# A 5x5 depthwise convolution split between GpSimd, beside the attention, and VectorE and TensorE, ahead of it

## What is computed

```python
xn = layer_norm(x, ln1_g, ln1_b)
q, k, v = xn @ q_w + q_b, (xn @ k_w + k_b) * scaling, xn @ v_w + v_b
lepe = dwconv(v, lepe_w, lepe_b)          # depthwise, 5 x 5, 'SAME', one filter per channel
qr, kr = theta_shift(q, sin, cos), theta_shift(k, sin, cos)   # 12 heads of 8 channels
attn = softmax(einsum("bnld,bnmd->bnlm", qr, kr) + mask)      # L = 1024 tokens
o = einsum("bnlm,bnmd->bnld", attn, v) + lepe
x = x + (o @ out_w + out_b)
```

## Time and profile before

| what | us |
|---|---|
| median of three runs | 3670.02 |
| the three runs | 3669.94, 3670.02, 3678.01 |
| the profiled execution, its own time | 3670.32 |
| its span, first to last instruction | 3668.7 |
| v projections, before the convolution (from 195.2) | to 219.95 |
| `depthwise` for `lepe` | 220.2 to 297.3 |
| attention, with its start and end | 297.9 to 1050.5 |

### The profile page before, as it was taken

How to read it: one execution, slowest core, us unless ns; L and a number is a source line. 1 busy time by engine, 2 the same in 40 slices (tenths; PEclk the granted TensorE clock), 3 DMA queues, 4 the chain that set the end, 5 groups by cost and what they waited for, 6 DMA issues and landing times. The chain is left out here.

```text
span 3668.7 us, 136690 instructions
## 1 busy us (share of the span) xinstructions
PE 3141.9 (86%) x50394; PEld 2339.4 (64%) x50394; DVE 2582.0 (70%) x12076; ACT 1821.7 (50%) x5594; POOL 583.8 (16%) x2420
## 2 busy tenths in 40 slices
PE   5378999999958947999999999999999998577787
PEld 1134666566622315888988888889888887254454
DVE  4567999999974635777777777777777778466562
ACT  2215999999933025444544444444444445133342
POOL 0001111111100001222222222222222222111110
PEclk9678999999978966555555555555555555678888
DMA  1312333333330000000000000000000000000000
GB/s 32 108 47 95 108 107 107 107 107 107 108 91 1 10 7 2 5 5 5 5 5 5 5 5 5 5 5 5 5 5 5 5 5 4 11 1 1 0 5 13
DMA packets 54608, 116.12 MB, mean 32 GB/s; under 512 B 12313, under 2 KB 19801, under 8 KB 53692
## 3 DMA queue, kind: packets, MB, share of 16 engines
q1 hardware_dynamic: 37104, 53.42, 5.3%
q0 software_dynamic: 13824, 50.34, 3.9%
q10 hardware_dynamic: 2956, 3.15, 0.4%
HBM read 84.06 MB, written 22.81 MB: 29 GB/s over the span
## 5 line engine op out<-in xcount | busy, mean ns | idle before, releaser
L504 PE MATMUL g_zr<-g_hp,g_wp 97*128 97x4 f16 x24576 | 1082.6, 171 | 53.4 <-issue 49.0
L504 PEld LDWEIGHTS g_zr<-g_hp,g_wp 97*128 97x128 f16 x24576 | 956.4, 108 | 157.4 <-issue 51.3
L595 ACT ACTIVATE g_e<-g_tn 96x8 f32<-96x8 f32 x2048 | 437.0, 213 | 557.8 <-DVE g_tn L540 557.8
L480 PE MATMUL g_zr<-s_inner,g_wi 96*128 (+2 forms) x6240 | 585.1, 234 | 61.9 <-issue 39.7
L612 POOL COPY s_y<-g_hs 96x8 f32 x2048 | 401.0, 196 | 1374.9 <-DVE g_hs L555 1374.9
L553 DVE TENSOR_TENSOR_SCAN g_hp<-g_gates,g_e 96x16 f16<-96x16 f32 x2048 | 382.1, 187 | 316.7 <-ACT g_e L595 207.6
L592 ACT ACTIVATE g_gates<-g_zr 96x16 f32<-96x16 f32 x2048 | 399.5, 195 | 315.5 <-PE g_zr L504 315.4
L511 PE MATMUL g_n<-g_hp,g_wp 97*128 97x8 f16 x8192 | 520.1, 174 | 0.0
L844 DVE CUSTOM_DVE_ANT_0 a_negated<-a_scores,a_mask 128x1024 f32<-128x1024 f32 x384 | 468.0, 1219 | 59.1 <-PE a_scores L762 41.2
L870 ACT ACTIVATE a_probs<-a_negated,a_negmax 128x1024 f32<-128x1024 f32 x384 | 442.4, 1152 | 26.1 <-DVE a_negmax L844 16.3
L540 DVE TENSOR_TENSOR_SCAN g_tn<-g_gates,g_n 96x24 f32<-96x24 f32 x2048 | 387.8, 189 | 95.7 <-ACT g_gates L592 95.7
(11 more groups left out here) (324 smaller groups left out, 3058.5 us busy)
## 6 DMA issues: line engine op xcount, KB each, us to landing
a_mask<-in_L_mask POOLq DMA_DIRECT2D x96, 512.0 KB, 5.6
a_k<-k_rows SPq DMA_DIRECT2D x96, 144.0 KB
q_rows<-r_q_parts SPq DMA_DIRECT2D x12, 576.0 KB, 7.4
k_rows<-r_k_parts SPq DMA_DIRECT2D x12, 576.0 KB, 7.4
a_q<-q_rows SPq DMA_DIRECT2D x96, 72.0 KB
o_parts<-a_o_sb SPq DMA_DIRECT2D x384, 18.0 KB
o_part<-o_parts SPq DMA_DIRECT2D x32, 192.0 KB
out_x<-x SPq DMA_DIRECT2D x4, 384.0 KB, 3.0
```

The costliest lines, as they stand in the source:

```text
L480: pe.matmul(o, wi[0:K, half, pw, d * NG + g, :], x, start=first, stop=False, skip_group_check=True)
L504: mm = pe.matmul(zr_bank[u, k][:, 1 - g, d, :, at], wp[0:97, part, (2 * u + d) * NG + g, :], hp[u][0:97, d * NB:(d + 1) * NB, e], start=False,
L595: act.activation(e1[u][:, :, 0], tn[u][:, :, 2], ACT.Tanh, scale=to_tanh).then_inc(n_and_zh[u], 1)
```

## The change

The convolution's work is divided anew, by image.

- **Images 2 and 3** stay in `depthwise`, ahead of the attention: of their four half images two go to TensorE (`on_tensor` is 2), and image 2 goes to VectorE.
- **Images 0 and 1** (`BESIDE`): ScalarE starts `lepe` with bias and centre tap (12) by an ACTIVATE for each, at the end of the token stage. The other 24 taps are done by GpSimd inside the attention, one tap of one image in each group whose image is 0 or 1: 48 groups, `convolve(2 * h + half, b, g)`. Each is a TENSOR_SCALAR into `term` and a TENSOR_TENSOR that adds it to `lepe`, with a wait between (`convolved`).
- GpSimd's `v` copy of a group waits for the convolutions of the groups before it, and its twelve heads are all written out, where ten ran in a loop.
- `vpad` and `lepe_w` are kept in memory through the attention.

The diff, cut to its core:

```diff
-def depthwise(nc, tag, jobs, size, on_tensor):
+def depthwise(nc, tag, jobs, size, on_tensor, batch=tuple(range(NB))):
-    work = [(k, b, half) for k in range(len(jobs)) for b in range(NB) for half in range(2)]
+    work = [(k, b, half) for k in range(len(jobs)) for b in batch for half in range(2)]
...
+BESIDE = (0, 1)
+OTHER_TAPS = [tap for tap in range(25) if tap != 12]
...
                         po.sem_inc(v_may, 1)
+                        po.wait_ge(convolved, done(g))
                         po.tensor_copy(vs[b % 2][:, :, 0:8], head).then_inc(v_ok, 1)
                         if b == 1 and not (half == 0 and first) and not (last and half == 1):
                             mask_load(h if half == 0 else h + 1, 1 - half, True)
-            heads(po, body)
+                        if b in BESIDE:
+                            convolve(2 * h + half, b, g)
+
+            def done(g):
+
+                return 2 * sum(i % NB in BESIDE for i in range(g))
+
+            def convolve(n, b, g):
+
+                tap = OTHER_TAPS[n]
+                dy, dx = tap // 5, tap % 5
+                image = lepe[:, cols(b)].rearrange("c (y x) -> c y x", y=HH)
+                po.wait_ge(v_ok, g + 1)
+                po.tensor_scalar(term[:, :, :], vpad[:, b, dy:dy + HH, dx:dx + HH], lepe_w[:, tap:tap + 1], None,
+                                 ALU.mult).then_inc(convolved, 1)
+                po.wait_ge(convolved, done(g) + 1)
+                po.tensor_tensor(image, image, term[:, :, :], ALU.add).then_inc(convolved, 1)
+
+            for h in range(NH):
+                body(h, h == 0, h == NH - 1)
...
                             act.activation(vt[:, i // 2, (i % 2) * 4:(i % 2) * 4 + 4, :], tokens[i % 2][:, :, 0:C],
                                            ACT.Copy).then_inc(taken, 1)
+                    for b in BESIDE:
+                        act.activation(lepe[:, cols(b)].rearrange("c (y x) -> c y x", y=HH),
+                                       vpad[:, b, 2:2 + HH, 2:2 + HH], ACT.Identity, bias=v["L0_lepe_b"][:, :],
+                                       scale=lepe_w[:, 12:13])
-                depthwise(nc, "r_lepe", [(vpad, lepe_w[:, :], v["L0_lepe_b"][:, :], None, lepe)], 5, 3)
+            depthwise(nc, "r_lepe", [(vpad, lepe_w[:, :], v["L0_lepe_b"][:, :], None, lepe)], 5, 2,
+                      tuple(b for b in range(NB) if b not in BESIDE))
```

More of the change, by code:

```diff
@@ L275, in _ @@
                 padded, taps, bias, addend, out = jobs[k]
-                images = [(b, HALF * sum((k, b, half) in own for half in range(2))) for b in range(NB)]
+                images = [(b, HALF * sum((k, b, half) in own for half in range(2))) for b in batch]
                 images = [(b, rows) for b, rows in images if rows]
@@ L619, with attention @@
 LAG = 2
-def attention(nc, mask, q_rows, k_rows, v_tokens, o_parts):
+BESIDE = (0, 1)
+OTHER_TAPS = [tap for tap in range(25) if tap != 12]
+def attention(nc, mask, q_rows, k_rows, v_tokens, o_parts, vpad, lepe, lepe_w):
     with ExitStack() as ctx:
@@ L639, in attention @@
         ident = sb("ident", [128, 128])
+        term = sb("term", [C, HH, HH])
+        convolved = sem("convolved")
         scores = [ctx.enter_context(nc.psum_tensor(f"a_scores{i}", [128, L], F)) for i in range(2)]
@@ L995, in retention_block @@
         lepe = outer.enter_context(nc.sbuf_tensor("r_lepe", [C, N], F))
+        lepe_w = outer.enter_context(nc.sbuf_tensor("r_lepe_w", [C, 25], F))
+        vpad = outer.enter_context(nc.sbuf_tensor("r_vpad", [C, NB, HH + 4, HH + 4], F))
         vt = outer.enter_context(nc.sbuf_tensor("r_vt", [128, NB, 8, C], F))
@@ L1095, in retention_block @@
                     sends += 3 * NB
[L1097 to L1110, removed]
-                    def _(pe):
-                        for i in range(N // BANK):
-                            if i >= 2:
-                                pe.wait_ge(taken, i - 1)
-                            for k in range(4):
-                                t = i * BANK + k * 128
-                                mm = pe.matmul(tokens[i % 2][:, k, 0:C], xn[:, t:t + 128], vw[:, :], start=True,
-                                               stop=True)
-                            mm.then_inc(made, 1)
-                    @block.scalar
-                    def _(act):
-                        for i in range(N // BANK):
-                            act.wait_ge(made, i + 1)
-                            act.activation(vt[:, i // 2, (i % 2) * 4:(i % 2) * 4 + 4, :], tokens[i % 2][:, :, 0:C],
-                                           ACT.Copy).then_inc(taken, 1)
-                depthwise(nc, "r_lepe", [(vpad, lepe_w[:, :], v["L0_lepe_b"][:, :], None, lepe)], 5, 3)
@@ L1131, in _ @@
                     sp.wait_ge(sent, 16 * sends)
-        attention(nc, d["L0_mask"], q_rows, k_rows, vt, o_parts)
+        attention(nc, d["L0_mask"], q_rows, k_rows, vt, o_parts, vpad, lepe, lepe_w)
         recycle(nc)
```

28 lines of the change are left out of this document (27 added, 1 removed).

## The result

The changed kernel takes **3638.26 us** (median of four runs, 3638.13 to 3641.11), the kernel before, run beside it, 3669.98 (four runs, 3667.72 to 3678.01). The ratio is 0.9912, its 95% interval 0.9894 to 0.9929. 12 us are missing from the sum.

What follows compares the result with a forecast made beforehand. The prediction took TensorE to bound `depthwise`, and TensorE, VectorE and ScalarE in a ring to bound the attention. Terms -21.8 and +2.2, others 0, sum to -19.6 against 3670.3; from the median 3670.0 it forecast 3650.4 us, range 3645 to 3672.

Steps and rivals of the forecast that it cites:

- The half image: In `depthwise`, TensorE does two half images instead of three, so its last eviction comes 21.78 us earlier: -21.8 us.
- The two ACTIVATEs: At the token stage's end, ScalarE starting images 0 and 1 holds the barrier: +2.2 us, bounds 1.95 and 2.30.
- The clock term: At the start of `depthwise`, TensorE's low-clock stretch after idling stays as costly: 0, bounds -3.1 and +3.1 us.
- VectorE did not come last: In `depthwise`, VectorE's image 2 takes at most 34 us against TensorE's 55; late only past 2.1 us a tap.
- GpSimd's pairs cost 0: In the attention, 48 pairs of 3.8 us each, at most 4.9, fit GpSimd's free time: 0 us.
- Rival A: In the attention, GpSimd's pairs hold back VectorE's custom instruction, 2.3 us a pair, 110 us: 3760 us; chance 0.12.
- B: In the attention, GpSimd is too slow and values come late; at 20 us a pair 3963 us; chance 0.02.
- C: In the attention, q loads come late more often beside the mask's traffic: +15.8 us, 3666 us; chance 0.05.
- D: In the attention, every pair costs someone 0.2 to 0.5 us, 17 us in all: about 3667 us; chance 0.08.
- a TENSOR_SCALAR at 1.28 us: In GpSimd's pair, the TENSOR_SCALAR costs as much as an AFFINE_SELECT, 1.28 us, at most the TENSOR_TENSOR's 2.36.
- GpSimd keeps up in each group: In the attention, GpSimd has 4.0 of 7.5 us to do without the mask, 6.1 with it, 7.2 at the bound.
- the second step: In the attention, a `v` copy queued behind a pair may be 9.8 us late, so a pair must exceed 17 us.

Runs made afterwards that it cites:

- the kernel with both paddings: The changed kernel with all four images on GpSimd, plus 50 tiny products on TensorE and 75 one-column instructions on VectorE at the attention's start: 3571.3 us.
- two half images on TensorE: The kernel before with two instead of three of eight half images on TensorE, VectorE taking six, GpSimd as before: 3658.27 us, ratio 0.9965.
- all beside without padding: The changed kernel with all four images' taps on GpSimd beside the attention and no `depthwise` block for `lepe`: 3587.0 us, ratio 0.9764.

## Why the prediction was right in direction and too small

**Right, by its own steps.** The half image was worth 21.8 us. The two ACTIVATEs end at 221.26 + 2.39 = 223.65, and the last token eviction ahead of them at 221.37, so they hold the barrier for 2.28 us; 2.2 had been taken. TensorE's first product shows them too: it was at 228.03 and is at 231.72, 3.7 us later, of which 1.4 are this execution's later start. The clock term, taken as 0 within -3.1 and +3.1, was -1.1: the low stretch held 3.9 us of products instead of 6.1, where "about 6" had been named as a sign of being right, and the first eviction came 23.96 instead of 25.03 us after the first product. -21.8 + 2.3 - 1.1 = -20.6, and the stage shows -20.5. VectorE did not come last: it took its 24 taps in 31.56 us, 1.3 each with the wait, where lateness began at 2.1.

**Right: GpSimd's pairs cost 0.** Rival A asked whether the custom instruction, with one input in PSUM, meets a tensor instruction of GpSimd. It does not: its median is 1221 ns beside 48 pairs and 1220 before, and 1220 in mean beside 96 in the kernel with both paddings; the kernel without the pairs takes the same time as the one with them. The Trainium skill's rule of the shared ports ("SBUF — State Buffer", Who interferes with whom), which exempts an instruction with an input in PSUM, agrees with that. B did not come: no pair reached the 17 us from which it decides. C did not come: the trace after shows no wait for q, where before had three with 1.8 us in all. D did not come: a group takes 7.5 us with a pair and without.

**Mis-sized, but off the path.** I took a TENSOR_SCALAR at 1.28 us, from an AFFINE_SELECT with as many elements, and set the upper bound at the TENSOR_TENSOR's 2.36. It takes 2.87, outside my bounds; the pair with its waits takes 5.35 us where I had taken 3.8 and bounded by 4.9. I had said that GpSimd keeps up in each group; in the one with the mask's DMAs it falls 0.6 us behind. What saved the term was the second step, that a copy may be 9.8 us late. The mistake was to think that one input must be cheaper than two. The Trainium skill ("GPSIMD Engine Reference", Engine selection) has the same thought, one-input work as roughly at line rate; this trace disagrees, with 2.87 us against 2.38 for the TENSOR_TENSOR.

**The step that failed** is in the sum itself. It counted the stages whose work changes, and took 0 for all others without saying why. I wrote of the attention that "no other engine's code in the attention is changed", and that was right; but I never asked what the shorter code does behind it. The changed number of instructions was in plain view: 75 products of L265 before and 50 now. What was not looked at is that the longest stage by far, 1680 us of a loop that goes back 15 times, had TensorE idle for "issue" for 49.0 + 39.7 = 88.7 us, with nothing to wait for in the program. Such time depends on something that isn't in the program's logic, and so it may change with any edit. In its place the runs showed: TensorE's place in the code -27, VectorE's place +14.4, together -12.9 to the loop's measure. With it the stage table closes: -20.5 - 12.9 = -33.4, and the other four stages give +1.1 back before rounding, a difference of spans of 32.3.

Could it have been predicted? VectorE's part not, from the profile of before alone: it has no stop at the turn there, and nothing shows that it may get one. TensorE's part perhaps, in hindsight: its second stop comes after only 0.71 us of work, so the loop starts shortly before the end of a piece, and less code ahead of it leaves more of the loop in that piece. The bound could have been had from the waits in any case: 39.7 us to be won. An honest range would have been wider, downward above all.

**What stays open.** The attention's main part takes 726.3 us in before and 726.2 with two half images on TensorE, and 723.3 to 724.7 in all others. These two are the kernels in which TensorE's matmuls wait for q, 1.8 and 1.6 us in all (0.5 at most in the others), which is most of the attention's -2.2; why the waits come in these two was not found. That TensorE's second stop ends with a fetch rests on the 16 KB packets, which end 1.2 to 1.8 us ahead of it at every turn of the kernels in which it shows, and on the padding; for VectorE's stop the trace does not tell which packets are its own. The paddings tried fit a period of 64 products but don't exclude 32. The loop of all beside without padding is 15 us shorter than before's; TensorE's stops are 9.9 us shorter in sum (49.6 + 29.2 against 88.7), VectorE's small waits are gone, and what the rest is made of was not measured, nor is it more than loops of one place differ by. VectorE's code was tried at few places, with a stop at the turn for 50 instructions fewer alone, so its period was not measured.

## What to carry to other kernels

Work that nobody needs before a stage's end is free on an engine that idles through it, as long as it can be cut into pieces that fit between that engine's duties: here up to 571 of 730 us of GpSimd's time, at no cost that the runs show to a ring of three engines in which TensorE is busy for 99%. Before summing up a change, list the "issue" waits of every loop in the program, also of those that it does not touch: here they moved with the length of the code ahead of them, and made 40% of the gain. And compare variants by stage, since a difference in the total may belong to the place of the code and not to the idea; a few tiny instructions as padding tell the two apart.

## What was not expected of the hardware

- The stops of a loop that goes back depend on where the code lies: TensorE's second stop is 1.95 to 2.65 us or about 0.7, VectorE's 1.55 us or none, 15 times each; 39 tiny products ahead of the loop bring 27.7 us (one run), 64 bring nothing (one run).
- TensorE goes on from the second stop 3.1 to 3.4 us in mean after it went on from the first, with 0.71, 1.46 or 2.5 us of work between them.
- The two engines' stops don't add up: with TensorE's second stop in place, a loop with VectorE's shorter code took 1683.1 us against 1680.0; without it VectorE's was worth 14.4 us.
- A TENSOR_SCALAR of [96, 1024] float32 on GpSimd takes 2.79 to 2.87 us, with a constant or a factor from memory, from a window or from one piece; a TENSOR_TENSOR of the same size takes 2.38.
- The first TENSOR_SCALAR of the program, behind the configuration instruction, started 0.11 us after the copy ahead of it had ended:

```profile
287.50 0.25 POOL L749 COPY a_v<-r_vt 128x64 f32<-128x64 f32 x1
287.86 2.85 POOL L765 TENSOR_SCALAR a_term<-r_vpad,r_lepe_w 96x1024 f32<-96x1024 f32 x1
```
